# Moving GpSimd's DMA issues, splitting the first weight load, and moving layer 2's first six heads as three and three

## The reference, cut to what matters

```python
x = x + attention_rel(_gn(x))        # layer 0: 12 heads of 16, relative position terms
x = x + rope_block(_gn(x))           # layer 1: layer norm, rope, attention, layer norm, GELU feed-forward
x = x + neighbourhood(_gn(x))        # layer 2: 7x7 neighbourhood mask, 16 register keys and values
x = x + attention_rel(_gn(x))        # layer 3: as layer 0
```

## Time and profile before

| | |
|---|---|
| median of 3 runs | 158.56 us (157.37 to 159.72) |
| the profiled execution | 159.08 us |
| its span, first to last instruction | 156.4 us |
| TensorE busy | 141.6 us, 91% of the span |
| TensorE weight loads busy | 94.2 us, 60% |
| VectorE busy | 91.1 us, 58% |
| ScalarE busy | 70.7 us, 45% |
| GpSimd busy | 53.1 us, 34% |
| layer 0 ends / layer 1 ends / layer 2 ends | about 38 / 92.5 / 121 us |

### The profile page before, as it was taken

How to read it: one execution, slowest core, us unless ns; L and a number is a source line. 1 busy time by engine, 2 the same in 40 slices (tenths; PEclk the granted TensorE clock), 3 DMA queues, 4 the chain that set the end, 5 groups by cost and what they waited for, 6 DMA issues and landing times.

```text
span 156.4 us, 2663 instructions
## 1 busy us (share of the span) xinstructions
PE 141.6 (91%) x920; PEld 94.2 (60%) x920; DVE 91.1 (58%) x239; ACT 70.7 (45%) x164; POOL 53.1 (34%) x94
## 2 busy tenths in 40 slices
PE   6989589999898958999999999968999999999992
PEld 2569366645457836755458865756666478676550
DVE  2775368736734988876541026666634845697462
ACT  4474127761233216682137713417571445167810
POOL 7689988840200289930000000720000047600000
PEclk9999999999999999999999999999999999999999
DMA  3907648999200156820000000450000017620001
GB/s 84 260 19 184 196 123 262 275 295 298 64 2 0 51 168 96 169 41 0 4 0 0 0 0 2 146 156 4 0 0 0 0 49 212 171 82 0 0 0 50
DMA packets 12508, 13.55 MB, mean 87 GB/s; under 512 B 4144, under 2 KB 10336, under 8 KB 12496
## 3 DMA queue, kind: packets, MB, share of 16 engines
q1 hardware_dynamic: 7792, 9.29, 21.0%
q0 software_dynamic: 3472, 3.01, 8.6%
q10 hardware_dynamic: 1232, 1.08, 2.4%
HBM read 6.82 MB, written 0.20 MB: 45 GB/s over the span
## 4 chain that ended last, share of the span: by engine, by line
PE 62%; DMA 9%; POOL 7%; ACT 7%; DVE 6%; issue 4%; SPq 3%; DVEq 0%; POOLq 0%; ACTq 0%
PE PC L1056 14%; PE RING L1031 9%; PE RING L917 4%; PE RING L995 4%; DMA KS<-KL 4%; PE PA L1066 4%; PE RING L1260 3%; DMA WQKV<-in_w 3%; PE PB L1066 3%; PE PB L995 2%; ACT PR L634 2%; DMA QS<-COLL 2%; SPq L329 2%; PE PA L1266 2%; PE PB L1266 1%
## 5 line engine op out<-in xcount | busy, mean ns | idle before, releaser
L634 ACT ACTIVATE PR<-RING 128x512 f32<-128x512 f32 (+1 forms) x48 | 25.7, 553 | 9.3 <-PE RING L1031 9.1
L917 PE MATMUL RING<-WARM 128*128 128x512 bf16 x84 | 24.7, 406 | 1.3 <-POOL WARM L388 1.3
L1056 PE MATMUL PC<-PR,VX 128*32 128x256 f32 (+1 forms) x192 | 23.6, 369 | 0.1
L827 DVE TENSOR_REDUCE NM<-RING 128x2 fp32r<-128x512 f32 (+1 forms) x32 | 20.1, 652 | 4.1 <-PE RING L995 3.9
L1031 PE MATMUL RING<-QS,KS 128*128 128x256 f32 (+1 forms) x96 | 20.2, 305 | 0.3 <-ACT QS L626 0.2
L1031 PEld LDWEIGHTS RING<-QS,KS 128*128 128x128 f32 x96 | 13.9, 188 | 7.7 <-issue 4.5
L626 ACT ACTIVATE QS<-PA 4x512 fp32r<-4x512 f32 (+1 forms) x20 | 10.6, 531 | 16.5 <-PE PA L1009 16.5
L430 POOL DMA_DIRECT2D QS<-QL x2 | 1.1, 550 | 43.0 <-DVE QL L778 31.0
L827 DVE TENSOR_REDUCE NM<-PB 128x2 fp32r<-128x512 f32 (+1 forms) x16 | 10.5, 654 | 5.6 <-PE PB L995 5.5
L1056 PEld LDWEIGHTS PC<-PR,VX 128*32 128x32 f32 x192 | 8.6, 109 | 8.4 <-ACT PR L634 1.8
L995 PE MATMUL RING<-KS,QS 128*128 128x256 f32 (+1 forms) x64 | 13.2, 298 | 0.0
(11 more groups left out here) (189 smaller groups left out, 271.6 us busy)
## 6 DMA issues: line engine op xcount, KB each, us to landing
WQKV<-in_w SPq DMA_DIRECT2D x2, 576.0 KB, 8.5
WO<-in_wo SPq DMA_DIRECT2D x4, 288.0 KB, 8.8
W<-in_ff SPq DMA_DIRECT2D x2, 576.0 KB, 9.6
KS<-KH ACTq DMA_DIRECT2D x10, 96.0 KB, 3.1
WQKV<-in_w SPq DMA_DIRECT2D x2, 432.0 KB, 5.3
QS<-QHL POOLq DMA_DIRECT2D x12, 64.0 KB, 2.6
KS<-KL SPq DMA_DIRECT2D x8, 96.0 KB, 3.1
QS<-QH SPq DMA_DIRECT2D x8, 96.0 KB, 2.3
```

The source lines that it names most:

```text
L634: A(PR[:, h % NPR, 0:n], exponents(l, h)[:, 0:n], ACT.Exp).then_inc(sem("probs"), 1)
L827: V.tensor_reduce(NM[:, TURN_OF[h], :, h % GH], MAXIMA[h % 3][:, 0:2 * n_keys].rearrange("p (q k) -> p q k", q=2), AX.X, ALU.max, negate=T ...
L917: M(bank, WARM[:, 0:P], WARM[:, :], start=True, stop=True)
L1056: ins = M(columns(h)[:, reach(l, k)], VX[:, k, h, :], half(PR[:, h % NPR, :], l, k), start=(k == 0 and l != 2), stop=(k == 1), skip_group_ ...
```

## The change

- Start: `w0` is loaded as two DMAs, first the query columns ("w0q"), then `vecs`, then key and value columns ("w0"). The query projection waits for "w0q" alone. Two leading `keep_warm` matmuls and the one between the two group statistics go in layer 0. `HOT_HALF` goes from 6 to 4, so ScalarE copies four heads of hot rows and VectorE eight.
- GpSimd, layer 0: the ones load comes right behind the scaling of `w0`. Two of the five clears (ONESC and VR) go behind the column term moves.
- Layer 1: QL of chunk 0 is issued by SP and not by POOL. The register key moves go from POOL (12) to SP (18, since chunk 0 is cut in two), behind SP's other moves of the layer. POOL's mask loads thus follow its subtraction directly.
- Layer 2: the channels of chunk 0 are stored as two groups of three heads. Before head 0 only the moves of heads 0 to 2 are needed. Heads 3 to 5 ("next heads", "next rows") are waited for in front of head 3. POOL issues eight moves in place of two: QL and KH of the first three heads; QL, KH, KH and KL of the next three ("next rows"); and QL and KL of chunk 1 ("later rows"), which SP issued before.

The diff, cut to what the above needs:

```diff
-HOT_HALF = NH // 2
+HOT_HALF = NH // 3
...
-        loads = [("x", X, "xT"), ("gavg", GAVG, "gavg"), ("vecs", VECS, "vecs"), ("w0", WQKV[0], "w0"), ("hot", HOT, "hot"),
+        loads = [("x", X, "xT"), ("gavg", GAVG, "gavg"), ("w0q", WQKV[0][:, :, 0:Q2], "w0q"), ("vecs", VECS, "vecs"), ("w0", WQKV[0][:, :, Q2:Q2 + 2 * C], "w0"), ("hot", HOT, "hot"),
...
-                if l not in REL_LAYERS:
+                if l == 2:
+                    for first, done in ((0, "q stack"), (THREE, "next heads")):
+                        for block in (Q_HIGH, Q_AGAIN):
+                            move("qh", rows_of(queries, block)[:, first:first + THREE], QH[three_rows(first), 0, :], done, 1)
+                        if first == 0:
+                            move("kl", rows_of(KS, Q_AGAIN, KEY0, REG1)[:, 0:THREE], KL[three_rows(0), 0, :], "k stack", 1)
+                    for block in (Q_HIGH, Q_AGAIN):
+                        move("qh", rows_of(queries, block)[:, HPC:NH], QH[:, 1, :], "later heads", NC)
+                    continue
+                if l == 1:
...
-                        if i:
-                            move("ql", rows_of(queries, Q_LOW)[:, heads], QL[:, i, :], "later heads", i + 1)
+                        move("ql", rows_of(queries, Q_LOW)[:, heads], QL[:, i, :], "later heads" if i else "q stack", i + 1)
                         move("kl", rows_of(KS, Q_AGAIN, KEY0, REG1)[:, heads], KL[:, i, :], "later heads" if i else "k stack", i + 1)
+
+                    sync.wait_ge(sem("kr parts"), 2)
+                    for col in (0, REG1):
+                        for block, src in ((Q_HIGH, KRH), (Q_LOW, KRH), (Q_AGAIN, KRL)):
+                            for heads, rows in ((slice(0, THREE), src[three_rows(0), 0, :]),
+                                                (slice(THREE, HPC), src[three_rows(THREE), 0, :]), (slice(HPC, NH), src[:, 1, :])):
+                                sync.dma_start(rows_of(KS, block, col, col + NREG)[:, heads].bitcast(F32), rows.bitcast(F32))\
+                                    .then_inc(sem("kr stack"), 16)
                     continue
...
-            for n, (tile, value) in enumerate((
-                    (VX[:, :, :, :], 1.0), (NM[:, 0:3].bitcast(F32), 0.0),
-                    (NM[:, 3:6].bitcast(F32), 0.0), (ONESC[:, :], 1.0 / C), (VR[:, :, :], 0.0))):
-                g.memset(tile, value).then_inc(sem("backgrounds"), 1)
-                pool.wait_ge(sem("backgrounds"), n + 1)
-
             pool.wait_ge(sem("hot rows"), 2)
             pool.dma_start(KS[0:GH, :, KEY0:REG1 + NREG], a["ones"]).then_inc(sem("one rows"), 16)
+
+            background(1, VX[:, :, :, :], 1.0)
+            background(2, NM[:, 0:3].bitcast(F32), 0.0)
+            background(3, NM[:, 3:6].bitcast(F32), 0.0)
...
+                move("ql", 1, rows_of(QS[l % 2], Q_LOW)[:, threes], QL[three_rows(0), 0, :], "first rows")
+                move("kh", 1, rows_of(KS, Q_LOW, KEY0, REG1)[:, threes], KH[three_rows(0), 0, :], "first rows")
+                move("ql", 1, rows_of(QS[l % 2], Q_LOW)[:, nexts], QL[three_rows(THREE), 0, :], "next rows")
+                for block in (Q_HIGH, Q_LOW):
+                    move("kh", 1, rows_of(KS, block, KEY0, REG1)[:, nexts], KH[three_rows(THREE), 0, :], "next rows")
+                move("kl", 1, rows_of(KS, Q_AGAIN, KEY0, REG1)[:, nexts], KL[three_rows(THREE), 0, :], "next rows")
+                move("ql", NC, rows_of(QS[l % 2], Q_LOW)[:, later], QL[:, 1, :], "later rows")
+                move("kl", NC, rows_of(KS, Q_AGAIN, KEY0, REG1)[:, later], KL[:, 1, :], "later rows")
...
                     pool.wait_ge(*upto("scores", 0, NH))
-                    pool.wait_ge(sem("kr parts"), 2)
-                    for col in (0, REG1):
...
-                keep_warm(free, (7, 3, 3, 3)[l])
+                keep_warm(free, (5, 3, 3, 3)[l])
...
+                if h == THREE and l == 2:
+                    pe.wait_ge(*upto("next heads", l, signals["next heads"][l]))
+                    pe.wait_ge(*upto("next rows", l, signals["next rows"][l]))
```

More of the change, by code:

```diff
@@ L284, in build @@
                     "qh": {0: NG, 1: NC, 2: NC, 3: NG}, "ql": {0: NG, 1: NC, 2: NC, 3: NG},
-                    "q stack": {l: (5 if l in REL_LAYERS else 2) * 16 for l in range(LAYERS)},
+                    "q stack": {0: 5 * 16, 1: 3 * 16, 2: 2 * 16, 3: 5 * 16},
                     "k stack": {l: (3 if l in REL_LAYERS else 2) * 16 for l in range(LAYERS)},
-                    "later heads": {l: (1 if l in REL_LAYERS else 4) * 16 for l in range(LAYERS)}}
+                    "later heads": {0: 16, 1: 4 * 16, 2: 2 * 16, 3: 16},
+                    "next heads": {2: 2 * 16}, "next rows": {2: 4 * 16}, "later rows": {2: 2 * 16}}
         signals |= {"later keys": {l: 2 * 16 for l in range(LAYERS)},
-                    "first rows": {l: (4 if l in REL_LAYERS else 2) * 16 for l in range(LAYERS)}}
+                    "first rows": {0: 4 * 16, 1: 16, 2: 2 * 16, 3: 4 * 16}}
         signals |= {"x": {l: 3 * NC if l == 1 else NC for l in range(LAYERS)}, "sums": {0: 1}}
@@ new lines, in _, with move @@
+            background(1, VX[:, :, :, :], 1.0)
+            background(2, NM[:, 0:3].bitcast(F32), 0.0)
+            background(3, NM[:, 3:6].bitcast(F32), 0.0)
+            def move_first_rows(l):
+                if l == 1:
+                    pool.wait_ge(*upto("kh", l, 1))
+                    pool.dma_start(rows_of(KS, Q_LOW, KEY0, REG1)[:, 0:HPC].bitcast(F32), KH[:, 0, :].bitcast(F32))\
+                        .then_inc(sem("first rows"), 16)
+                    return
+                def move(signal, count, stack, src, done):
+                    pool.wait_ge(*upto(signal, l, count))
+                    pool.dma_start(stack.bitcast(F32), src.bitcast(F32)).then_inc(sem(done), 16)
+                threes, nexts, later = slice(0, THREE), slice(THREE, HPC), slice(HPC, NH)
+                move("ql", 1, rows_of(QS[l % 2], Q_LOW)[:, threes], QL[three_rows(0), 0, :], "first rows")
[6 more added lines that the diff above has]
+                move("kl", NC, rows_of(KS, Q_AGAIN, KEY0, REG1)[:, later], KL[:, 1, :], "later rows")
@@ L584, in move_keys @@
                 heads = slice(i * HPC, (i + 1) * HPC)
+                rows = slice(0, CC)
+                if l == 2 and i == 0:
+                    heads, rows = slice(0, THREE), three_rows(0)
                 for block in (Q_HIGH, Q_LOW) if i else (Q_HIGH,):
-                    act.dma_start(rows_of(KS, block, KEY0, REG1)[:, heads].bitcast(F32), KH[:, i, :].bitcast(F32))\
+                    act.dma_start(rows_of(KS, block, KEY0, REG1)[:, heads].bitcast(F32), KH[rows, i, :].bitcast(F32))\
                         .then_inc(sem("later keys" if i else "k stack"), 16)
@@ L981, in for_maxima @@
                 s = MAXIMA[h % 3]
+                if h == THREE and l == 2:
+                    pe.wait_ge(*upto("next heads", l, signals["next heads"][l]))
+                    pe.wait_ge(*upto("next rows", l, signals["next rows"][l]))
+                if h == HPC and l == 2:
+                    pe.wait_ge(*upto("later rows", l, signals["later rows"][l]))
                 if h == HPC:
@@ L1132, in _ @@
                     ready = upto("ni", 1, NC)
-                loaded(pe, f"w{l}")
+                loaded(pe, f"w{l}" if l else "w0q")
                 if l in REL_LAYERS:
@@ L1283, in qk_order @@
     def qk_order(l, w):
-        by_head = order_turned if l == 1 else order
+        by_head = (order, order_turned, order_threes, order)[l]
         q = w[..., np.tile(order2, (1, 2)).reshape(Q2)] if l in REL_LAYERS else w[..., by_head]
```

25 lines of the change are left out of this document (13 added, 12 removed).

## The result

The changed kernel took 163.77 us (median of 4 executions, 163.15 to 164.58). Runs of the kernel before beside it gave 158.86 us. The ratio is 1.0322, with a 95% interval of 1.0226 to 1.0419. So the change costs about 5 us, where I had forecast 159.2 us and a range up to 160.8. The profiled execution of after took 164.58 us with a span of 162.5. That is 6.1 us more span than before has.

A forecast was written before the change was run, and what follows sets the result against it. TensorE's own order was taken to bound the kernel, with 5.7 us of large DMA waits as the most to gain. Layer 0 -0.3, layer 1 +0.7 and layer 2 +0.2 gave +0.6: 158.56 to 159.2 us, range 157.2 to 160.8.

The forecast's parts named there:

- Layer 1, head 6: Before head 6 of layer 1: early masks share the DMA engines with KL, which lands at 61.9, not 61.19; layer 1 +0.7.
- the bounds: KL's landing in layer 1: as before or even in 2.3 us below; all mask packets first, +3.4, above.
- the nearest row: A layer 0 KL issued near 18.2 among moves of all three queues, 3.8 us; 3.9 taken for layer 1's KL.
- rival 3: Layer 1: all four mask loads pass ahead of KL, +3.4 - 0.2 there, 161.7 us in all; chance 0.06.
- held by one mask load: Layer 1, by the skill's queue rule: KL held about one mask load, an estimated 0.85 us; layer 1 +0.65.
- Layer 1, head 0: Head 0 of layer 1 starts near 56.8 on SP's KL, 0.4 earlier; the gain is lost at head 6.
- Layer 0: Start up to head 0: POOL's shorter queue gives -0.4, VectorE's longer cast beside the scaling costs 0.1; -0.3.
- a delay of the projections: Layer 0: TensorE's 2.42 us wait before COLL lands covers a projection delay of up to this length.
- Rival 4: Layer 0: w0's second half lands late, the scaling waits for the whole cast; +0.8, 160.3 us; chance 0.08.
- Layer 2: Head 0 starts a second earlier, but head 3 waits for POOL's "next rows" and loses it; +0.2.
- Rival 2: Layer 2: POOL's six issues don't bound head 3, which starts 1.0 earlier; -0.6 in all, 158.0 us; chance 0.08.
- Rival 1: Layer 1: masks cost KL nothing, it lands in 2.9 us; -0.9 in all, 157.7 us; chance 0.33.

The follow-up runs named there:

- run 1: The changed kernel, but POOL issues the four mask loads only after layer 1's chunk 1 moves have landed: 158.70 us, ratio 0.9928.
- run 5: The kernel before, with POOL's four mask loads issued ahead of its 12 register moves and no move given to SP: 161.46 us, ratio 1.0197.
- run 2: The kernel before with the layer 1 edits alone (SP issues QL and 12 register moves, masks early): 163.52 us, ratio 1.0257.
- run 7: The changed kernel with 15 warm matmuls in front of the waits at head 6 of layer 1: 163.21 us, ratio 1.0278.
- run 8: The changed kernel with late masks as in run 1, but layer 2 unsplit as before: 159.33 us, ratio 1.0032.
- run 9: Run 1 with layer 2's KL of heads 3 to 5 issued by SP and one KH by ScalarE: 161.66 us, no ratio given.
- run 10: The kernel before with the layer 1 edits alone and the mask loads behind two waits for chunk 1's moves: 158.68 us, ratio 1.0008.
- run 11: Run 10 with four more warm matmuls in front of head 0 of layer 0: 158.52 us, ratio 1.0000.
- run 4: The kernel before with the layer 0 start edits alone (w0 split, hot rows, clears moved, fewer warm matmuls): 158.22 us, ratio 1.0042.
- run 3: The kernel before with layer 2's split alone (first six heads as two parts of three): 159.03 us, ratio 0.9987.
- run 6: The changed kernel with two mask loads early and two after chunk 1's moves have landed: 161.07 us, ratio 1.0144.

## Why the prediction was wrong

**Layer 1, head 6: the step that failed.** The mechanism was the forecast's: the masks come among the moves of chunk 1, KL lands later, and TensorE waits over 1 us on it at head 6. The term was mis-sized. Of the bounds, 2.3 us and +3.4 on top of some 2.9, I took 3.9, "the nearest row", a KL of layer 0 among moves of all three queues. That row has no 192 KB loads beside it. Measured were 5.45 us. The number to use stood in the prediction: the masks fill all engines for 3.4 us. Of that, KL paid 3.2 us with all four early (5.4 against the 2.2 of run 1), and 2.8 to 3.7 over runs 5, 2 and 7. The queues between KL's issue and its landing in after (60.09 to 65.54; packets, MB, share of 16 engines) show the same:

```profile
q0 software_dynamic: 811, 0.77, 68.2%
q1 hardware_dynamic: 786, 0.32, 28.7%
q10 hardware_dynamic: 223, 0.20, 13.5%
```

q0 is POOL's queue: it is absent from the same view of run 1, where POOL issues nothing between KL's issue and landing. It moved 0.77 MB in this time, nearly all of the 4 x 192 KB (0.79 MB).

The reason I gave against rival 3, that KL is issued before the last two mask loads, failed in its premise: three loads, and not two, were issued before KL, and the fourth followed it by 0.2 us (58.70 + 3 x 0.54 = 60.3 against 60.09). How much the fourth cost is not shown. KL's issue was not the miss. Counted from the start of the layer it is at 19.49 and was at 19.82, 0.3 earlier where 0.2 was forecast, though SP's QL issue took 0.82 us. Head 6 started 25.03 us into the layer and not at 22.92, which is +2.1 where +0.7 was forecast, and the landing, 1.55 us over the 3.9 that I took, covers the difference of 1.4.

The Trainium skill (DMA: Bandwidth & Descriptors, "Queues, rings and completion order") says that a DMA engine goes round its queues and takes a packet from each. The trace agrees that the queues share the engines: all three move bytes in the stretch above. That KL is held by one mask load was my own step from it, and it doesn't hold: with two loads KL was held by 1.9 us and with four by 2.8 to 3.7. I had counted KL alone, but it stood in SP's queue behind QL, which was held too (4.9 us to its landing in after, 2.6 in run 1), and POOL's queue moved more than twice the bytes of SP's.

**The clock: a term that was missing.** I had read a granted clock of 1.00 in all stretches of before and had no term for a fall. Behind the 3.21 us wait it fell to 0.50 for 3.4 us. By run 7 this costs 1.45 us, so layer 1 lost 3.6 us: 2.1 at head 6 and 1.5 by the clock. In layer 0 of the profiled execution it fell for 6.8 us more, before any mask load is issued.

**Layer 1, head 0: right.** Head 0 came 0.5 to 0.6 earlier in the runs (0.4 forecast), and its releaser is KL as forecast. I said this gain doesn't last, because of head 6. With late masks it does last, together with the 0.57 us of the earlier trace rows: head 6 then starts 21.8 us into the layer, 1.1 earlier, and layer 1 is 53.6 us in all five kernels that have it (runs 1, 8, 9, 10, 11), 1.1 less than before. Whether it lasts to the end of the kernel stays open, since run 1 won 0.7% with the doubt given there, and run 10 nothing.

**Layer 0: wrong, and small.** The forecast was -0.3 by POOL's queue, with the first QHL issue at 11.9 and COLL's at 16.4. They came at 12.32 and 16.86 in after, and at 12.06 and 16.81 in run 4. From the end of the scaling to the first QHL issue it took 2.9 us in both, where 2.8 was forecast and 3.2 was before, so that term was nearly right. The rest was not: the scaling lasted 1.95 us and not 1.80, and in after it also started 0.3 later, since the second half of w0 landed later (7.31 against 7.01). In runs 1 and 4 the slower projections came on top. I had written that TensorE's 2.42 us of wait cover a delay of the projections. But the data of COLL are made from them, and those were early by only the 1.35 us by which POOL's queue was late.

What covers it all is COLL's landing. In five kernels whose layer 0 has no edit (before, runs 2, 3, 5 and 10) it took 2.1 to 3.6 us. Rival 4 occurred only in its beginning, the later w0. The scaling started at 7.46 and the cast at 7.75, and neither waited for the other.

**Layer 2: right in mechanism.** These were forecast: head 0 one us earlier, then a new wait of about 1 us at head 3 ended by POOL's KL. They came as 0.75 earlier and a wait of 1.05 us. Head 3 is 0.4 later than in before where 0.2 was forecast, and the stage is 0.3 longer. Rival 2 is refuted by runs 3 and 8, and run 9 shows that the queue of POOL isn't the only thing in the way.

**The rivals' chances.** Rival 1 (the masks cost KL nothing, chance 0.33) is refuted by runs 1, 5 and 6. What it said of POOL's small moves fits: without them and without masks beside it KL lands in 2.2 us and not in 3.0 (runs 1 and 10). Rival 3 (all masks go first, 161.7 us) was nearly the true mechanism, with 3.2 of its 3.4 us, and had a chance of 0.06. Its own point of decision was badly drawn: not "all four pass before KL", but each adds its share. With the measured terms in its place the sum closes: the profiled 159.08 + 3.6 (layer 1 with its clock) + 0.3 (layer 2) + 0.2 to 2.3 (layer 0, without and with a fall of the clock) = 163.2 to 165.3, where the four executions had 163.15 to 164.58. The top is 0.7 over the profiled 164.58, since that execution took 2.1 us more than its span and that of before 2.7; the spans alone close (156.4 + 6.2 = 162.6, measured 162.5). The 0.2 is a rough value: layer 0 of run 4 ended 0.2 earlier than that of before, and of run 1 0.3 later.

## What to carry to other kernels

When a bulk load moves forward in time, price it at its full DMA time against every small move still in flight or issued behind it, unless a row shows otherwise: here KL paid 2.8 to 3.7 us for loads that fill all engines for 3.4. Put a wait for the urgent moves in front of it: here two waits brought layer 1 from 58.3 to 53.6 us. And when issues move earlier, look at whether the data that they carry are still early enough, as the COLH issue of run 1 shows. A wait of two or three us on TensorE should be counted with the clock that may fall behind it, and an edit under 1% should be judged by its stage as well as by the total, because landings in stages without any edit move the total by as much.

## What the hardware showed that I had not expected

- The granted clock fell to half behind waits of TensorE of 3.21 us (after, layer 1) and 3.26 us (run 2), but not behind 2.00 us (run 6). It also fell behind one of 2.47 us (run 5). In run 2 it fell during the wait, at 63.0. Behind head 0 of layer 0 it fell after a wait of 1.83 us in after, 1.93 in run 10 and 2.8 in runs 2 and 3, and it stayed at 1.00 after 2.42 us in before and 1.84 in run 9. So the length of the wait alone doesn't decide. These are the windows of after there:

```profile
21.00:22.00 1.00, 0.65 (x5) 0.40 (x4) 1.00 (x3) 0.31 (x1) 0.73 (x4) 0.61 0.53 144
22.00:28.00 6.00, 5.90 (x27) 4.76 (x28) 3.57 (x7) 2.81 (x6) 5.09 (x10) 0.50 0.64 184
28.00:29.00 1.00, 1.00 (x9) 0.55 (x8) 0.87 (x2) 0.96 (x2) 0.80 (x2) 0.97 0.78 223
```

- A fall in layer 0 also comes without the change. Run 3, which has the start of the kernel before, has it too (0.50 from 22 to 25), and of 23 executions of the kernel before beside run 10, 8 had a mean clock of 0.989 or less, with spans of 156.0 to 157.9, and 15 had 0.997 or more, with 155.1 to 156.2. What decides whether it falls is open, and so is why it lasted 6.8 us in after and 3.4 in runs 2, 3 and 10.
- COLL's landing in layer 0 took 3.26 us before, 2.54 and 2.86 us in after and run 4, and 2.1 and 3.64 us in runs 5 and 3, whose layer 0 is that of before. A forecast that moves its issue by 0.3 us can't be told from that.
